# Two-layer cross attention: the opening and the batch ends of the second attention joined, and its tokens turned inside the first MLP's last weight group

## The chip, the cores and the metric

The kernel runs on one core of one Trainium2 chip. The metric is the device time of one launch in microseconds (us), lower is better. The core has five engines that run side by side and meet at semaphores: TensorE (PE; its weight loads are shown apart as PEld), VectorE (DVE), ScalarE (ACT), GpSimd (POOL) and SyncE (SP), whose queue issues most of the DMAs.

## The reference, cut to what matters

Four batches (B = 4) of 512 tokens with 512 features, a context of 64 tokens per batch, 16 heads of 32 features, all in float32. Two layers follow each other.

```python
# layer 0: tokens attend to the context, then an MLP
q = layer_norm(x) @ q_w + q_b;  k, v = ctx @ k_w + k_b, ctx @ v_w + v_b
x = softmax(mask(q k^T * HD**-0.5)) v @ cproj_w + cproj_b + x
x = x + gelu(layer_norm(x) @ fc_w + fc_b) @ proj_w + proj_b
# layer 1: the tokens are queries, keys are tokens AND context (512 + 64)
h = concatenate([latents, context]);  q = latents @ q_w + q_b;  kv = h @ kv_w + kv_b
attn = softmax(mask(q k^T / HD)) v            # one row sum per head and query
a = attn @ out_w + out_b + latents
out = gelu(rmsnorm(a) @ mlp_w1 + mlp_b1) @ mlp_w2 + mlp_b2 + latents
```

The latents of layer 1 are the tokens that layer 0 leaves. Both attention and MLP need them with the features on the partitions ("turned"), because PE sums over partitions.

## The kernel before, in words

The program is written engine by engine: each of the five has its own instruction stream, the orders are written out by hand, and semaphores tie them together. Each runs four stages: attention 0, MLP 0, attention 1, MLP 1. Every large product is made of three half products: an operand is split into a high part (`fp32r`) by ACT and a low part by DVE (`split_lo`, L1289), and high by high, high by low and low by high are summed in one PSUM bank. So a projection of a 128-row block is 12 matmuls of 512 columns (4 blocks of features by 3), and an evacuation of a bank is one ACT instruction and then one DVE instruction.

**MLP 0** goes through four groups of 512 hidden features; inside a group it goes through the four batches. A batch of a group is eight blocks of 12 matmuls: `fc1(0) fc1(1) fc2(0) fc1(2) fc2(1) fc1(3) fc2(2) fc2(3)`, 96 matmuls. Sums are kept in SBUF for all batches (`acc_`). Group 0 is written out batch by batch, with the norm and the turning of the next batch between the blocks (`turn_mlp`, 12 times four transposes); groups 1 to 3 are loops over the batches. When a batch of group 3 is done, SP stores its tokens to memory (`after_layer0`).

**Attention 1, opening** (before its loop): the tokens of batch 0 are in SBUF again; PE turns them (`nT0` to `nT3`, four transposes each) and the context (`nC`), projects queries, keys and context keys of head groups 0 and 1 (`nQ0 nK0 nKC0 nQ1 nK1 nKC1`) and the values (`nV0` to `nV4`). Queries and keys go through memory: SP stores the two parts (`q_parts`, `k_parts`) and loads them stacked, 32 rows per part, with a row of ones or of the mask beside them (`stack`). DVE sets the constant rows with memsets (L1629 to L1632). Then 20 `max_step`s find the row maxima of head group 0: a matmul to one of two banks and a DVE reduction from it. `max_turn` turns the maxima, SP moves them to a row of the queries (`max_row`), and the first scores can start.

**Attention 1, a batch**: four head groups (c = 0 to 3), each of 20 steps. A step has one score matmul, two exps on ACT (high and full), the low part on DVE or POOL, and two value matmuls four steps later. Between them stand the `max_step`s of the next head group and the "fillers": the projections for the head group after next. In c = 1 the fillers also hold `nT0` to `nT3` and `nC` of the next batch, at steps 12, 13, 15, 18 and 19. Batches 0 to 2 are one loop, batch 3 stands behind it.

**Batch end**: PE projects the next batch's values (`nV0` to `nV4`; the first two between the last value products). The 16 rows of sums, which SP has moved to `s16`, are inverted by one DVE reciprocal of 16x512; four matmuls (`B0` to `B3`, L2043) spread the inverses over the features; DVE multiplies (L1612), ACT adds the value bias in place (L1161), ACT and DVE split the result by blocks of tokens (L1165, L1289), and `O0` to `O3` (L2049, 48 matmuls) project it. In batch 3 the turning of MLP 1's first batch takes the place of the `nV`s.

All `n..`, `B` and `O` results share two PSUM banks in turn: result n waits until result n-2 has been evacuated (`free`). The order of results is the list from `results`.

## Time and profile before

| | |
|---|---|
| median of 3 runs | 1812.98 us (1812.66 to 1815.59) |
| the profiled execution | 1810.96 us, of which the span of its instructions is 1809.1 us |
| PE busy | 1623.9 us (90% of the span), 6993 matmuls |
| DVE, ACT, POOL busy | 1010.0, 699.9, 543.4 us |
| mean granted TensorE clock | 0.944 of full speed |

The share of busy time is a mean over stages with different limits, and PE's busy time is modelled: a matmul of 512 columns that stands alone is counted at about 0.4 us, in a stream its start follows the one before by 0.23 us. So the stages have to be read from the timeline, by when one piece of work starts and the next one starts. In the trace attention 1 begins at about 696 us, its loop at about 757 us; batch ends begin at about 895, 1064, 1236 and 1395 us.

### The profile page before, as it was taken

The page shows a single profiled execution, that of the slowest core. Times are in us where ns is not written, and L with a number is a line of the kernel's source. Part 1 is how long each engine was busy: PE and PEld are TensorE (multiplying, and loading weights), DVE is VectorE, ACT ScalarE, POOL GpSimd, SP SyncE. Part 2 cuts the span into 40 slices and gives each one's busy share as a digit, 9 for nine tenths or more (in the row PEclk, how much of TensorE's full clock was granted, in tenths as well). Part 3 has the DMA queues.
Part 4 walks back from the last instruction along what each step waited for, and adds up shares of the span by engine and source line. Part 5 has one row for each costly group of instructions (what it writes and reads, how often), then busy time and mean ns, then how long its engine had stood idle before and what let it go on. Part 6 is the DMA issues. An engine that isn't in the chain of part 4 may idle for free.

```text
span 1809.1 us, 23113 instructions
## 1 busy us (share of the span) xinstructions
PE 1623.9 (90%) x6993; PEld 1214.7 (67%) x6993; DVE 1010.0 (56%) x1612; ACT 699.9 (39%) x1260; POOL 543.4 (30%) x543
## 2 busy tenths in 40 slices
PE   5778897899999998899988998999887899999998
PEld 4667775677878786565655656665553577787886
DVE  3665565664333335488757866785877465333332
ACT  3433333341111111277557746673767232111111
POOL 3231236404040413234414423341457220404000
PEclk9888898999999998799989999899987799999999
DMA  5012013501010223423222322231222320101011
GB/s 181 1 36 70 23 51 125 191 13 47 0 47 0 68 96 120 130 84 109 82 71 78 111 63 103 71 106 59 91 86 71 139 77 12 35 12 35 0 47 46
DMA packets 60730, 126.13 MB, mean 70 GB/s; under 512 B 10397, under 2 KB 10722, under 8 KB 60642
## 3 DMA queue, kind: packets, MB, share of 16 engines
q1 hardware_dynamic: 53602, 102.08, 17.0%
q0 software_dynamic: 7040, 23.07, 4.1%
q8 instruction: 31, 0.51, 0.1%
q14 instruction: 57, 0.47, 0.1%
HBM read 90.25 MB, written 34.60 MB: 69 GB/s over the span
## 4 chain that ended last, share of the span: by engine, by line
PE 72%; DVE 13%; issue 7%; ACT 5%; DMA 2%; SPq 1%; POOL 1%; DVEq 0%; ACTq 0%; POOLq 0%
PE bank L2078 19%; PE bank L2090 18%; PE bank L1952 5%; DVE RA L1289 4%; PE bank L1948 3%; PE bank L2049 3%; DVE FA L1522 3%; PE bank L2002 3%; PE bank L1987 3%; PE bank L2003 2%; PE bank L1965 2%; PE bank L1774 2%; PE bank L1750 2%; PE bank L1969 2%; PE bank L1825 1%
## 5 line engine op out<-in xcount | busy, mean ns | idle before, releaser
L2090 PE MATMUL bank<-W,RA 128*128 128x512 f32 x1536 | 379.7, 399 | 5.9 <-DVE RA L1289 5.7
L2078 PE MATMUL bank<-RA,W 128*128 (+1 forms) x1536 | 374.8, 396 | 2.8 <-issue 2.3
L2090 PEld LDWEIGHTS bank<-W,RA 128*128 128x128 f32 x1536 | 287.2, 189 | 78.1 <-DVE RA L1289 10.7
L2078 PEld LDWEIGHTS bank<-RA,W 128*128 128x128 f32 x1536 | 286.9, 188 | 74.9 <-issue 6.0
L862 POOL TENSOR_TENSOR RA<-FA,RA 128x512 fp32r<-128x512 f32 (+1 forms) x160 | 216.0, 1354 | 392.9 <-ACT FA L1125 392.6
L1289 DVE TENSOR_TENSOR RA<-FA,RA 128x512 fp32r<-128x512 f32 (+2 forms) x308 | 273.3, 889 | 46.3 <-ACT FA L1125 32.6
L1181 ACT ACTIVATE FA<-bank,cols 128x512 f32<-128x512 f32 x128 | 88.1, 688 | 541.5 <-PE bank L2078 541.4
L1652 DVE CAST RA<-FA 128x512 fp32r<-128x512 f32 x128 | 62.8, 491 | 354.3 <-ACT FA L1181 354.3
L1124 ACT ACTIVATE RA<-bank 128x512 fp32r<-128x512 f32 (+1 forms) x320 | 193.6, 605 | 142.1 <-PE bank L1987 138.1
L1522 DVE TENSOR_REDUCE FA<-bank 128x1 f32<-128x512 f32 x256 | 169.1, 685 | 57.7 <-PE bank L1965 56.9
L1125 ACT ACTIVATE FA<-bank 128x512 f32<-128x512 f32 (+1 forms) x320 | 193.3, 604 | 0.0
L1987 PE MATMUL bank<-RA 98*128 98x512 f32 (+1 forms) x320 | 140.8, 442 | 14.8 <-DMA RA<-rows_ 7.2
L1952 PE MATMUL bank<-RA,W 128*128 128x512 f32 (+1 forms) x576 | 145.3, 370 | 5.1 <-DVE FA L1512 3.0
L2002 PE MATMUL bank<-RA 128*65 128x512 f32 (+1 forms) x320 | 136.9, 428 | 10.3 <-POOL RA L862 5.2
L1289 DVE TENSOR_TENSOR RA<-bank,RA 128x512 fp32r<-128x512 f32 (+1 forms) x124 | 82.9, 680 | 111.2 <-ACT RA L1105 43.0
L2003 PE MATMUL bank<-RA 128*65 128x512 f32 (+1 forms) x320 | 131.4, 411 | 0.0
L1952 PEld LDWEIGHTS bank<-RA,W 128*128 128x128 f32 x576 | 98.3, 197 | 40.5 <-issue 12.7
L721 POOL TENSOR_TENSOR W<-raw,W 128x512 fp32r<-128x512 f32 (+1 forms) x88 | 110.4, 1255 | 7.3
L1687 DVE TENSOR_TENSOR FA<-bank,FA 128x512 f32 (+1 forms) x128 | 86.8, 689 | 38.9 <-PE bank L2090 37.5
L1965 PE MATMUL bank<-RA 97*128 97x512 f32 x256 | 99.8, 430 | 6.4 <-DMA RA<-k_parts 2.0
L1987 PEld LDWEIGHTS bank<-RA 98*128 98x128 f32 (+1 forms) x320 | 60.1, 188 | 61.7 <-ACT FA L1125 35.2
L717 POOL TENSOR_SCALAR W<-raw 128x512 fp32r<-128x512 f32 (+1 forms) x88 | 56.4, 641 | 58.0 <-DMA raw<-in_L_xattn_mlp_w_dram 19.1
(149 smaller groups left out, 1828.7 us busy)
## 6 DMA issues: line engine op xcount, KB each, us to landing
RA<-k_parts SPq DMA_DIRECT2D x96, 144.0 KB
FA<-after_layer SPq DMA_DIRECT2D x12, 1024.0 KB, 6.1
RA<-q_parts SPq DMA_DIRECT2D x96, 128.0 KB
k_parts<-FA SPq DMA_DIRECT2D x16, 576.0 KB, 2.8
after_att<-FA SPq DMA_DIRECT2D x32, 256.0 KB, 2.1
q_parts<-FA SPq DMA_DIRECT2D x16, 512.0 KB, 2.7
raw<-in_L_xattn_mlp_w_dram POOLq DMA_DIRECT2D x32, 256.0 KB, 3.4
RA<-after_att SPq DMA_DIRECT2D x10, 512.0 KB, 6.9
```

The source lines that it names most:

```text
L862: pool.tensor_tensor(pl[0:m, r, :], pf[0:m, r, :], ph[0:m, r, :].bitcast(F32), ALU.subtract).then_inc(p_lo_pool, 1)
L1124: act.activation(ph[0:m, r, :], src, ACT.Exp, scale=SCALE1)
L1125: act.activation(pf[0:m, r, :], src, ACT.Exp, scale=SCALE1).then_inc(p_exp, 1)
L1289: dve.tensor_tensor(dst, src, hi.bitcast(F32), ALU.subtract).then_inc(sem_, 1)
L1522: dve.tensor_reduce(nm_main[:, TT * j + t:TT * j + t + 1], bank[2 + i % 2][:, :], AX_X, ALU.max, negate=True).then_inc(mm_free, 1)
L1952: op = pe.matmul(dst[:, 0:m], W[:, "QK".index(kind[0]), a, k, c * P:(c + 1) * P], src[:, d, k, :], start=start, stop=stop)
L1965: pe.matmul(bank[2 + i % 2][:, :], QS[0:ROWMAX, c % 2, j, t * P:(t + 1) * P], KS[0:ROWMAX, c % 2, j, 0:S], start=True, stop=True).then_inc ...
L1987: pe.matmul(bank[4 + n % 2][0:m, :], KS[0:ROWMAX + 1, c % 2, j, t * P:t * P + m], QS[0:ROWMAX + 1, c % 2, j, :], start=True, stop=True).th ...
L2002: pe.matmul(o, v, ph[0:m, n % PRING, :], start=(t == 0), stop=False)
L2003: pe.matmul(o, v, pl[0:m, n % PRING, :], start=False, stop=(t == TT)).then_inc(pv_step, 1)
L2078: op = pe.matmul(bank[FC1_BANK[i]][:, :], W[:, slot, a, k, i * P:(i + 1) * P], yT_[:, ds(b * (2 * KT * S) + (d * KT + k) * S, S)], start=( ...
L2090: op = pe.matmul(bank[4 + t][:, :], gs[:, a, i, t * P:(t + 1) * P], W[:, slot + 1, d, i, :], start=(i == 0 and a == 0 and d == 0), stop=(i ...
```

## The change

Five edits in one:

1. The last group of MLP 0 is no longer a loop: its four batches are written out on PE, ACT and DVE. In batches 1 to 3 PE turns the tokens of the batch before, straight from `acc_` (`x_turn`, four times four transposes, between the blocks). Batch 0's turned tokens are split to where attention 1 reads them; those of batches 1 and 2 are copied out by ACT (`x_out`) and stored turned (`x_store`, to `x_turned`). Batch 3 is turned in the opening of attention 1.
2. In c = 1 of the loop `nT0` to `nT3` are no PE work: the tokens come from memory turned; ACT copies them to the high part and DVE makes the low part, both from SBUF, at steps 12 to 15, `nC` at 16. PE waits for them (`x_split`) only at `nQ0`.
3. The opening: the constant rows come by eight DMAs during MLP 0 (`constant_rows1`); the parts of `nQ0` go to memory before those of `nKC0` are there; the 20 `max_step`s stand between the halves of `nV0` to `nV3`, and `nV4` behind `max_turn`; GpSimd asks for the first value weights before it waits for MLP 0's end; ACT has one `Exp` of a single column ahead of it all.
4. The batch end: the sums of heads 0 to 11 (`EARLY` = 12) are inverted apart, in four pieces, those of heads 12 to 15 in one piece of 16 partitions; `B0` to `B3` stand between `nV2`, `nV3` and `nV4`; bias and split are one ACT and one DVE instruction per block of features; `O0` starts with the first three blocks of features.
5. Batch 3: the early inverses, `B0` to `B2` and their products stand inside the last steps of c = 3; two of the four turnings stand ahead of `O0`.

```diff
-        plan += [(s0, 1, f"nT{k}") for k, s0 in enumerate((12, 13, 15, 18))] + [(19, 1, "nC")]
+        plan += [(s0, 1, f"nT{k}") for k, s0 in enumerate((12, 13, 14, 15))] + [(16, 1, "nC")]
...
-    out += [] if last else [f"nV{t}" for t in range(TT + 1)]
-    return out + [f"B{k}" for k in range(KT)] + [f"O{t}" for t in range(TT)]
+    out += [f"B{k}" for k in range(KT)] if last else ["nV0", "nV1", "B0", "nV2", "B1", "nV3", "B2", "nV4", "B3"]
+    return out + [f"O{t}" for t in range(TT)]
...
+def first_max(t, part):
+    at = 2 * t + part
+    return range((5 * at + 1) // 2, (5 * (at + 1) + 1) // 2)
+FIRST_X = {"nKC0": (0, 1), "nK1": (2, 3)}
... SP, opening
+                sp.wait_ge(rows_set, 16 * 8 + ONE)
                 for c in range(2):
+                    sp.wait_ge(pb_free, use1(f"nQ{c}", first=True) + 1 + ONE)
+                    parts(0, 0, c)
+                    if c == 0:
+                        for half in range(2):
+                            stack(0, c, half, (0,))
                     sp.wait_ge(pb_free, use1(f"nKC{c}", first=True) + 1 + ONE)
-                    parts(0, 0, c)
                     parts(1, 0, c)
-                    sp.wait_ge(consts, 5 + ONE)
                     for half in range(2):
-                        stack(0, c, half)
+                        stack(0, c, half, (1,) if c == 0 else (0, 1))
+                    if c == 0:
+                        for k in range(KT):
+                            x_store(B - 1, k)
... SP, MLP 0, last group
                 for b in range(B):
-                    if b == 2 and L.index == 0:
+                    if b >= 2 and L.index == 0:
+                        for k in range(KT):
+                            x_store(b - 1, k)
+                    if b == B - 1 and L.index == 0:
                         first_inputs1()
+                        constant_rows1()
... ACT
+            def x_out(nb, k):
+                act.wait_ge(x_full, KT * nb + k + 1 + ONE)
+                src = bank[3 if nb < B - 1 else 2 + k % 2][:, :]
+                if nb == 0:
+                    act.activation(xT[:, 0, k, :], src, ACT.Copy).then_inc(x_hi, 1)
+                else:
+                    v = KT * (nb - 1) + k
+                    if nb < B - 1 and v > 1:
+                        act.wait_ge(x_stored[k % 2], 16 * (v // 2) + ONE)
...
+                    act.activation(x_stage[nb][k], src, ACT.Copy).then_inc(x_moved, 1)
...
+                act.activation(cols[:, NPAR + 3:NPAR + 4], cols[:, NPAR:NPAR + 1], ACT.Exp)
                 for u in split_by_act(FIRST):
+                    for k in FIRST_X.get(u, ()):
+                        x_out(B - 1, k)
                     hi(0, u, first=True)
... DVE, end of a batch of the loop
+                        inverse(0)
+                        inverse(1)
                         lo(b, "nV0")
+                        inverse(2)
+                        inverse(3)
                         lo(b, "nV1")
-                    o_sum(H - 1)
+                        o_sum(H - 1)
+                        for k in range(2):
+                            scaled(k)
+                            as_lo_(k)
+                            lo(b, f"nV{k + 2}")
+                        inverse_last()
+                        scaled(2)
+                        as_lo_(2)
+                        lo(b, "nV4")
+                        scaled(3)
+                        as_lo_(3)
... PE
+            def x_turn(nb, k):
+                if k == 0:
+                    pe.wait_ge(acc_added, (NGRP - 1) * B * TT + (nb + 1) * TT + ONE)
+                pe.wait_ge(x_moved, KT * nb + k - (nb == B - 1 and k > 0) + ONE)
+                for t in range(TT):
+                    at_t = nb * TT * D + t * D + k * P
+                    op = pe.transpose(bank[3 if nb < B - 1 else 2 + k % 2][:, t * P:(t + 1) * P],
+                                      acc_[:, at_t:at_t + P], ident[:, :])
+                op.then_inc(x_full, 1)
... PE, end of a batch of the loop, then of batch 3
+                        spread_inverse(0)
+                        project(b, "nV2", 0, 1)
+                        spread_inverse(1)
+                        project(b, "nV3", 0, 1)
+                        spread_inverse(2)
+                        project(b, "nV4", 0, 1)
+                        spread_inverse(3)
+                        output(0, range(KT - 1))
                     else:
                         wait_apart(pe, (mm_free, at(0, b, BSTEP, BSTEP)))
+                        turn_mlp(LAYERS[1], 0, 0, 2)
+                        turn_mlp(LAYERS[1], 0, 1, 3)
+                        output(0, range(KT - 1))
+                        spread_inverse(3)
+                        for u in range(2, 4):
+                            evacuated(LAYERS[1], 0, u - 1)
                             turn_mlp(LAYERS[1], 0, u, 2 + u % 2)
+                    output(0, range(KT - 1, KT))
+                    for t in range(1, TT):
+                        output(t, range(KT))
... PE, opening
+                for u in FIRST[:FIRST.index("nV0")]:
+                    for k in FIRST_X.get(u, ()):
+                        x_turn(B - 1, k)
                     project(0, u, 0, 1, first=True)
+                pe.wait_ge(consts, 5 + ONE)
+                pe.wait_ge(x_moved, KT * B + ONE)
+                for t in range(TT):
+                    for part in range(2):
+                        for i in first_max(t, part):
+                            max_step(0, 0, i)
+                        project(0, f"nV{t}", part, 2, first=True)
                 max_turn(0, "nR0", 0, 0, first=True)
+                project(0, f"nV{TT}", 0, 1, first=True)
... PE, MLP 0, a batch of the last group (b > 0)
                     fc1(0)
                     fc1(1)
+                    x_turn(b - 1, 0)
                     fc2(0)
+                    x_turn(b - 1, 1)
                     fc1(2)
+                    x_turn(b - 1, 2)
                     fc2(1)
+                    x_turn(b - 1, 3)
```

On ACT `x_out` 0 and 1 stand between the gelus 1 and 2 of the batch and `x_out` 2 and 3 between the gelus 2 and 3; on DVE, in batch 1 alone, the low parts of batch 0's tokens (`x_lo`) stand in the same places. On DVE in batch 3 the four early inverses stand at steps 12 to 15 of c = 3 and the products of `B0` to `B2` at steps 17 to 19.

## Rows read from the trace of the kernel before

**Rows 1.** The page's head: the span.

```profile
span 1809.1 us, 23113 instructions
```

**Rows 2.** Stretches of time: length, busy time by engine (instructions), granted clock, DMA share, GB/s.

```profile
315.00:421.00 106.00, 96.08 (x423) 73.33 (x422) 61.52 (x109) 39.13 (x62) 22.53 (x24) 1.00 0.25 87
...
609.00:696.50 87.50, 87.12 (x375) 69.60 (x374) 32.32 (x47) 11.02 (x16) 24.00 (x34) 1.00 0.24 81
696.50:757.20 60.70, 48.70 (x186) 34.53 (x184) 34.60 (x47) 9.04 (x16) 23.87 (x36) 0.80 0.52 166
```

**Rows 3.** Timeline of the opening: start, length, engine, instruction, [idle before, releaser].

```profile
696.26 1.03 PE L1929 MATMUL bank<-ident,FA 128*128 128x128 f32 x8
...
701.84 8.63 PE L1952 MATMUL bank<-RA,W 128*128 128x512 f32 x36 [0.98 <-DVE RA L1289]
...
703.60 0.35 SPq L622 DMA_DIRECT2D brow<-in_L_xattn_out_b_dram  x1
...
716.20 0.34 SPq L535 DMA_DIRECT2D q_parts<-FA  x1
...
719.37 0.69 ACT L1097 ACTIVATE FA<-bank,cols 128x512 fp32r<-128x512 f32 x1 [8.54 <-DMA q_parts<-FA]
...
723.80 14.21 PE L1948 MATMUL bank<-W,RA 128*128 128x512 f32 x60 [0.35 <-issue]
...
754.36 0.37 PE L1976 MATMUL bank<-ident,FA 128*16 128x128 f32 x1 [0.77 <-issue]
...
757.19 1.21 PE L1987 MATMUL bank<-RA 98*128 98x512 f32 x2 [2.47 <-DMA RA<-rows_]
```

**Rows 4.** ACT's groups by line: the table loads ahead of exps.

```profile
L1124 ACT ACT_TABLE_LOAD x4 | 5.1, 1283 | 46.8 <-PE bank L1987 46.8
...
L978 ACT ACT_TABLE_LOAD x1 | 1.3, 1283 | 2.5 <-issue 2.5
```

**Rows 5.** Stretches: c = 1 of batches 0 to 3, then c = 3 of batch 3.

```profile
788.40:824.00 35.60, 31.21 (x148) 20.76 (x148) 27.79 (x43) 25.82 (x52) 13.90 (x11) 1.00 0.25 80
...
955.50:993.20 37.70, 33.53 (x148) 22.86 (x148) 27.89 (x43) 25.86 (x52) 13.67 (x11) 0.91 0.23 75
...
1124.90:1165.00 40.10, 35.58 (x146) 24.11 (x146) 28.89 (x43) 25.92 (x52) 13.07 (x11) 0.83 0.22 70
...
1294.40:1328.10 33.70, 30.40 (x131) 19.70 (x131) 27.40 (x40) 24.51 (x48) 13.49 (x11) 0.95 0.26 84
...
1359.90:1395.00 35.10, 25.08 (x71) 11.09 (x69) 26.94 (x32) 26.86 (x52) 32.42 (x27) 0.81 0.15 54
```

**Rows 6.** PE's timeline in c = 1 of batch 2.

```profile
1155.09 1.12 PE L1929 MATMUL bank<-ident,FA 128*128 128x128 f32 x4 [1.65 <-DVE FA L1512]
```

**Rows 7.** DVE's groups, shapes apart, in c = 1 of batch 0: busy, mean ns.

```profile
L1289 DVE TENSOR_TENSOR RA<-FA,RA 128x512 fp32r<-128x512 f32 x9 | 8.5, 948 | 0.7 <-ACT FA L1125 0.6
...
L1289 DVE TENSOR_TENSOR RA<-bank,RA 128x512 fp32r<-128x512 f32 x3 | 2.0, 682 | 0.0
```

**Rows 8.** Timeline of the end of batch 0.

```profile
895.06 8.64 PE L1948 MATMUL bank<-W,RA 128*128 128x512 f32 x36
...
899.62 3.34 DVE L1592 RECIPROCAL FA<-FA 16x512 f32<-16x512 f32 x1
...
903.93 1.09 PE L2043 MATMUL bank<-FA,rows_ 16*128 16x512 f32 x2 [0.23 <-DVE RA L1289]
...
912.06 14.00 PE L2049 MATMUL bank<-W,RA 128*128 128x512 f32 x48 [3.19 <-DVE RA L1289]
...
925.90 0.63 PE L1987 MATMUL bank<-RA 98*128 98x512 f32 x2
```

**Rows 9.** Timeline of the end of batch 3 and the start of MLP 1.

```profile
1395.05 1.51 PE L1714 MATMUL bank<-ident,FA 128*128 128x128 f32 x8
...
1413.39 14.20 PE L2049 MATMUL bank<-W,RA 128*128 128x512 f32 x48 [3.14 <-DVE RA L1289]
...
1428.58 5.83 PE L2078 MATMUL bank<-RA,W 128*128 128x512 f32 x24 [0.98 <-issue]
```

More of the change, by code:

```diff
@@ L200, in at, with program @@
     return b * per + (base + max(n, 0) + ONE)
-def program(nc, x, ctx, mask_bool, mask_int, w, x1, xm, x2, q_parts, k_parts, out):
+def program(nc, x, ctx, mask_bool, mask_int, w, x1, xm, x2, q_parts, k_parts, x_turned, out):
     es = ExitStack()
@@ L1198, in mlp @@
                 for g in range(1, NGRP):
-                    with act.Fori(0, B) as b:
-                        batch(b, g, False)
+                    if L.index == 0 and g == NGRP - 1:
+                        for b in range(B):
+                            batch(b, g, False)
+                    else:
+                        with act.Fori(0, B) as b:
+                            batch(b, g, False)
             act.wait_ge(consts, 2 + ONE)
@@ L1691, in mlp @@
                 for g in range(1, NGRP):
-                    with dve.Fori(0, B) as b:
-                        batch(b, g, False)
+                    if L.index == 0 and g == NGRP - 1:
+                        for b in range(B):
+                            batch(b, g, False)
+                    else:
+                        with dve.Fori(0, B) as b:
+                            batch(b, g, False)
             attention0()
@@ L2018, in batch @@
                                 project(b, u, part, n, last)
+                            if not ahead and i >= 17:
+                                spread_inverse(i - 17)
                             if ahead and i == TURN:
@@ L2125, in mlp @@
                     pe.wait_ge(w_lo, L.before + L.units + (g + 1) * 2 * KT + ONE)
-                    with pe.Fori(0, B) as b:
-                        batch(b, g, False)
+                    if L.index == 0 and g == NGRP - 1:
+                        for b in range(B):
+                            batch(b, g, False)
+                    else:
+                        with pe.Fori(0, B) as b:
+                            batch(b, g, False)
             attention0()
```

292 lines of the change are left out of this document (189 added, 103 removed).

## The prediction

> **What bounds the kernel now.** I read the head first: the span is 1809.1 us [rows 1], the profiled execution 1810.96. That leaves 1.9 us outside the span, which I keep. The execution is 2.0 us under the median of 1812.98, so I add 2.0 at the end.
>
> Then the stretches. In the last group of MLP 0 PE is busy for 87.1 of 87.5 us at the full clock [rows 2]: there an added PE instruction costs its own time. The opening (696.5 to 757.2) is the opposite: 60.7 us, no engine busy throughout, clock at 0.80 on average [rows 2]. It is a chain of hand-overs, and the same holds for the batch ends [rows 8, 9]. The stages between are mixed: in c = 1 PE, DVE and ACT are all busy for 70 to 90% [rows 5]. So I price every edit by its stage, from "this starts" to "the next thing starts".
>
> **The change part by part.**
>
> *1. MLP 0, last group.* Three batches get four turns of four transposes, 12 turns. The opening shows two such turns in 1.03 us [rows 3], 0.52 each: 12 x 0.52 = 6.2. The copies on ACT (11.0 us busy in 87.5), the low parts on DVE (32.3) and the stores stand in engines that are mostly idle here [rows 2]; a turn waits for the copy of the one before, which has 12 matmuls to get done. What hides them is gone if a copy is late; then gelu 2 is late behind it. Written out instead of looped: I take nothing. Bounds: from 4 (turns that overlap the stream a little) to 18.5, the length by which group 0, which has 12 such turns and the norm, exceeds this one (106.0 against 87.5 [rows 2]). I take **+6**, as the added work has no norm.
>
> *2. Opening.* Before: MLP 0 ends at 696.26, projections start at 701.84, `q_parts` leaves at 716.20 because SP waits for `nKC0`, the values run from 723.80 to 738.01, the 20 max steps to 754.36, the first scores start at 757.19 [rows 3]. After: the context is turned at once, projections start at about 698.4 (estimate: one ACT, one DVE instruction). SP is free at 703.60, as it still waits for batch 3's store [rows 3]; `q_parts` follows, landing takes 3.2 (716.20 to 719.37), six loads to issue 2.7 (estimate, at 0.34 to 0.5 each), `k_parts` again 3.5, key loads and mask row about 4: 717.3. PE's own work to that point (24 full and 12 small matmuls, twice, 8.6 each [rows 3], and two pairs of turns, 1.03 each) ends at about 717 too. Max steps and `nV0` to `nV3` then share PE: alone they take 16.3 and 11.4 (4/5 of 14.21), so 16.3 if they overlap fully, 27.7 if not; I take 19, since half a value projection fits into the wait for a reduction. `max_turn` to first scores takes 2.8 [rows 3], and the low part of `nV3` is now queued on DVE ahead of it, 0.7 and a hand-over: 740.2. For stretches at the lower clock I add 2: 742.2 instead of 757.2, **-15**. The constant rows and the early dummy `Exp` lie under MLP 0's last matmuls; the value weights come about 3 earlier and are not waited for. Bounds: -20 (full overlap, no slow clock) to -5 (no overlap, load chain 2 later).
>
> *3. Table load.* In each round of the loop the first exp waits for a table load of 1.28 us after the scores are there; with one more after batch 3's square root that makes the four of [rows 4]. The `Exp` ahead of the loop makes the table the same on both ways into it. In attention 0 a loop of two rounds that is entered with the exp table has no load at its first exp: only the exp ahead of the loop has one (x1, [rows 4]). So three go: 3 x 1.28 = **-3.9**; bounds 0 and -3.9. The Trainium skill (ScalarE activation tables: per-element evaluation and per-set limits, section Table sets in the compiler and the runtime) says that loads are placed per block. Read strictly, the loop body is a block and keeps its load, and the term is 0; the row of attention 0 speaks against that reading.
>
> *4. c = 1.* The stage took 35.6, 37.7 and 40.1 in the three rounds; in batch 3, without `nT` and `nC`, 33.7 [rows 5]. PE stood still for up to 1.65 us ahead of an `nT` [rows 6], in order, so the scores behind it were late too, and in the third round the clock fell to 0.83. After, PE has only `nC`. ACT and DVE keep their instructions, so I don't take 33.7 but 34.0: 113.4 - 102 = **-11**. But the low parts now read two SBUF operands. Such ones took 948 ns here, those with one operand in PSUM 682 [rows 7]: 12 x 0.27 = 3.2 if all of it shows. Bounds: -12.3 (33.7 each) to +3.2 (no stall was on the path). The Trainium skill (SBUF — State Buffer, section Who interferes with whom) has the reason: a DVE instruction with two SBUF inputs excludes a GpSimd one that reads SBUF, and the later one stands still. By that the low parts of the probabilities on GpSimd would be late as well, which speaks against this edit.
>
> *5. Batch ends 0 to 2.* Before: 895.06 to 925.90, 30.8 us [rows 8]: `nV2` to `nV4` 8.6, the inverses spread after that, splits, 3.19 of waiting, `O` 14.0 at a clock that had partly fallen. The other two have the same pattern. After, on PE: 8.64 + four spreads of 1.09 + 48 matmuls at the pace of the 36 (0.24), 11.5: 24.5. Joined results wait for the bank of the result before last: its evacuation, ACT 0.69 and DVE 0.68 [rows 3, 7] with hand-overs 1.5, against one spread of 1.09 between, and DVE has products and splits in between: 0.6 ahead of each of `nV3`, `nV4`, `O0`, 1.9 in all: 26.4, that is -4.4 each, **-13.2**. The reciprocal of 3.34 becomes four quarters and one more of 0.84; the first two fill DVE's wait for `nV0`, the others that for `nV1`. Late next is the bank pair. Bounds each: -6.3 (no bank wait) to +4.2 (seven waits of 1.5 in full: 24.5 + 10.5).
>
> *6. Batch 3.* Before: 1395.05 to 1428.58, 33.5 [rows 9]. After: two turns 1.5; `O0` begins when ACT has done the last head and three splits (4 x 0.69) and DVE the last low part (0.7), with hand-overs at 1398.9, three matmuls more 1399.8; `B3` 1.1; the other two turns with an evacuation between 2.1: 1403.0; the remaining 39 matmuls at 14.20/48 = 0.30 each [rows 9] 11.5; the step to MLP 1 1.0: 1415.5, -13. In c = 3 DVE gets 3.34 + 3 x 0.68 = 5.4 more where it is busy for 26.9 of 35.1 us [rows 5]: 0 to 5.4, I take 2.5. **-10.5**; bounds -17 (full clock in `O`, DVE hidden) to 0.
>
> *Sum:* 6 - 15 - 3.9 - 11 - 13.2 - 10.5 = -47.6. 1810.96 - 47.6 = 1763.4, and with 2.0 to the median **1765**.
>
> **The rivals.**
>
> *A. The lock outweighs the stall in c = 1.* DVE and ACT already bound that stage; PE's stalls were slack, and the slower low parts add 3.2. For it: DVE is busy for 27 to 29 us there [rows 5]. Against: 33.7 in the round without `nT`. Then the term is +3.2 instead of -11: 1779.
>
> *B. The load stays in the loop.* 1765 + 3.9 = 1769.
>
> *C. Joining only trades one wait for another.* Two banks serve spreads, values and outputs; each waits out an evacuation, and the opening stays behind the load chain. Ends 0, opening -5, batch 3 -5: 6 - 5 - 3.9 - 11 - 5 = -18.9: 1794. For it: every joined result has the same two banks. Against: a spread or a projection always lies between two uses of a bank.
>
> *D. Slower: the last MLP group loses its clock.* Each turn waits for the sums of the batch before and for the copy of the last turn; if PE stands at them, the clock falls from 2.4 to 1.2 GHz as in c = 1 (0.83 in the third round [rows 5]), and a batch of some 22 us (87.5/4) takes 44. Three batches: +66, 1831. It decides from 47.6/22 = 2.2 batches on. Against: group 0 has 12 turns in the same places and a clock of 1.00 [rows 2].
>
> *E. The change moves the turns and saves none.* As many transposes come to MLP 0 as leave attention 1, and PE was the bound in both: part 4 gives 6.2 instead of 11: 1770.
>
> **How the numbers follow.** Forecast 0.60, A 0.13, B 0.09, C 0.08, D 0.03, E 0.07. The parts' bounds taken together are wider than I believe; the best ones that go together (4, -20, -3.9, -12.3, -18.9, -15) give -66 and 1747; I take 1745 as the low end. The high end reaches to C and stops short of D: 1792. The measurement can tell about 0.2% (3.6 us) from no change. Faster: all but D and a tail of C in which two terms turn positive, 0.94; within 0.2% 0.02; slower 0.04.
>
> **What would show it.** In the profile of the changed kernel: the last MLP group at 93 to 95 us and a clock of 1.00 (D wrong); from the last `fc2` to the first scores about 46 us, max steps and values interleaved over some 19; the first exp of each round without a load (B wrong); c = 1 at about 34 in every round with DVE's low parts of the tokens near 0.95 us (A wrong); the ends at about 26, with PE's waits ahead of `nV3`, `nV4` and `O0`; `O` in batch 3 ending some 12 us earlier behind the last value product. The prediction is wrong if the opening's load chain is later than 720, if PE waits at every spread, or if a turn in MLP 0 costs more than 1 us.

## The result, and the profile after

The kernel before took 1814.3 us (median of four runs beside the changed kernel, 1812.7 to 1817.5), the changed kernel 1783.7 (1781.7 to 1786.6): ratio 0.983, 95% interval 0.981 to 0.985. That is 30.6 us less, where 47.6 were forecast and 1765 us predicted. The profiled execution after took 1786.58 us, 24.4 less than the profiled one before.

The head of the page of the changed kernel, against [rows 1]:

```profile
span 1784.7 us, 23062 instructions
```

Two stretches of it, the last group of MLP 0 and the opening, with the columns of [rows 2] (length, busy time by engine, granted clock, DMA share, GB/s):

```profile
609.10:704.80 95.70, 95.24 (x434) 76.53 (x432) 35.74 (x53) 19.03 (x30) 25.73 (x38) 1.00 0.27 96
704.80:755.40 50.60, 39.31 (x186) 30.43 (x186) 19.67 (x36) 8.01 (x15) 22.71 (x34) 0.90 0.69 211
```

From its first to its last matmul the group took 90.3 us before ([rows 2] cuts some 3 us into it) and takes 95.6 now, 5.3 more, and PE stays at the full clock: rival D is out. The opening is 10.1 us shorter, with a DMA share of 0.69 instead of 0.52.

The opening on the timeline, against [rows 3]:

```profile
711.00 0.32 SPq L556 DMA_DIRECT2D q_parts<-FA  x1
...
714.56 0.28 DVE L1620 SCALAR_TENSOR_TENSOR FA<-bank,cols,FA 128x64 fp32r<-128x64 f32 x1 [1.01 <-ACT FA L1174]
...
715.88 2.96 SPq L567 DMA_DIRECT2D RA<-q_parts  x6
...
719.04 0.34 SPq L556 DMA_DIRECT2D k_parts<-FA  x1
...
725.10 1.25 SPq L567 DMA_DIRECT2D RA<-k_parts  x3
...
728.96 1.19 PE L2118 MATMUL bank<-RA 97*128 97x512 f32 x2 [6.98 <-DMA RA<-rows_]
...
751.00 0.27 PE L2129 MATMUL bank<-ident,FA 128*16 128x128 f32 x1
...
755.42 0.63 PE L2140 MATMUL bank<-RA 98*128 98x512 f32 x2
```

Read it backwards: the interleaved part takes 22.0 (728.96 to 751.00), and ahead of it PE stands for 7 us, waiting for the key loads and the constant row issued behind them. The key parts are ready on DVE at 714.84, but SP stores them only at 719.04: it first waits until the query parts have landed (4.9 us, not 3.2) and issues six query loads.

ACT's table loads ahead of exps, against [rows 4] (L1248 is the dummy, L1196 the exps of the second attention):

```profile
L1248 ACT ACT_TABLE_LOAD x1 | 1.3, 1283 | 0.0
L1196 ACT ACT_TABLE_LOAD x1 | 1.3, 1283 | 0.0
```

The one that is left at L1196 is the one behind batch 3's square root.

Stages c = 1 and c = 2 of the three rounds, cut at the issue of the row of maxima (`max_row`; the expectations below call it the mask row). They are shown in pairs because that row is later now, so that the cut itself moves:

```profile
783.12:820.46 37.34, 30.96 (x138) 19.69 (x138) 30.86 (x46) 29.16 (x59) 15.03 (x12) 0.99 0.24 76
820.46:852.81 32.35, 28.61 (x124) 19.48 (x124) 25.09 (x38) 21.43 (x42) 11.45 (x9) 0.91 0.40 120
948.79:984.92 36.13, 32.75 (x138) 20.21 (x138) 30.57 (x45) 28.11 (x57) 14.76 (x12) 0.93 0.26 78
984.92:1016.98 32.06, 28.59 (x125) 19.36 (x124) 24.55 (x38) 22.41 (x44) 11.47 (x10) 0.92 0.39 121
1112.78:1149.01 36.23, 32.93 (x138) 20.34 (x138) 30.59 (x45) 28.19 (x57) 14.79 (x12) 0.93 0.26 78
1149.01:1180.96 31.95, 28.51 (x125) 19.23 (x124) 24.54 (x38) 22.40 (x44) 11.47 (x9) 0.92 0.39 121
```

The same pair in the first round before:

```profile
787.88:823.45 35.57, 31.18 (x145) 20.42 (x146) 27.32 (x43) 25.79 (x52) 14.30 (x11) 1.00 0.25 80
823.45:854.69 31.24, 29.09 (x135) 19.19 (x133) 26.23 (x41) 24.29 (x49) 12.65 (x11) 1.00 0.38 124
```

The pairs sum to 69.7, 68.2 and 68.2 now; before they were 66.8, 68.9 and 71.5. PE has fewer instructions. DVE has 2.4, 1.4 and 0.4 us more than in the same round before, and c = 2, at the full clock in all rounds before, stands at 0.91 to 0.92. Two of PE's waits in the first round's c = 1 before (us in total, times, longest):

```profile
PE bank L1929 <- DVE FA L1512: 2.6, 2, 1.3
PE bank L1969 <- DVE FA L1522: 0.7, 1, 0.7
```

The same stage now, then c = 2:

```profile
PE bank L2122 <- DVE FA L1630: 2.0, 2, 1.4
```

```profile
PE bank L2140 <- DMA RA<-rows_: 3.0, 1, 3.0
```

PE's waits have moved. Those ahead of the turns (2.5 to 2.8 us a round) are gone, but the maximum steps (L2122, before L1969) wait longer for DVE's reductions, and the first scores of c = 2 wait for the row of maxima: 3.0, 1.6 and 1.6 us, at most 0.4 before. DVE's low parts with two SBUF operands, against [rows 7], c = 1 of the first round; the four of the tokens are among the 13:

```profile
L1386 DVE TENSOR_TENSOR RA<-FA,RA 128x512 fp32r<-128x512 f32 x13 | 12.1, 941 | 0.9 <-ACT FA L1197 0.9
```

The end of batch 0 on PE, against [rows 8], and that of batch 3, against [rows 9]:

```profile
893.14 1.12 PE L2175 MATMUL bank<-FA,rows_ 12*128 12x512 f32 x2
894.19 3.07 PE L2101 MATMUL bank<-W,RA 128*128 128x512 f32 x12
...
908.06 11.45 PE L2164 MATMUL bank<-W,RA 128*128 128x512 f32 x48 [0.61 <-DVE RA L1386]
919.34 0.63 PE L2140 MATMUL bank<-RA 98*128 98x512 f32 x2
...
1382.77 1.09 PE L1862 MATMUL bank<-ident,FA 128*128 128x128 f32 x8
...
1391.14 9.34 PE L2164 MATMUL bank<-W,RA 128*128 128x512 f32 x39 [0.35 <-issue]
...
1401.47 2.79 PE L2261 MATMUL bank<-RA,W 128*128 128x512 f32 x11 [0.98 <-issue]
```

The first takes 26.2 us (893.14 to 919.34; forecast 26.4, before 30.8), the second 18.7 (before 33.5).

### The profile page after: what moved, and what is told of

Same layout as the page of the kernel before. It is cut to its first block, busy times and chain, and to the rows that moved or that the text cites. A ratio compares the mean times of both kernels' runs of the same rounds, so it can differ in the third digit from the quotient of the medians.

```text
span 1784.7 us, 23062 instructions
## 1 busy us (share of the span) xinstructions
PE 1605.2 (90%) x7017; PEld 1198.8 (67%) x7017; DVE 1019.4 (57%) x1625; ACT 696.8 (39%) x1255; POOL 545.5 (31%) x543
## 4 chain that ended last, share of the span: by engine, by line
PE 71%; DVE 13%; issue 7%; ACT 4%; DMA 3%; SPq 1%; POOL 0%; DVEq 0%; ACTq 0%; POOLq 0%
PE bank L2261 18%; PE bank L2273 18%; PE bank L2105 5%; DVE RA L1386 4%; PE bank L2155 3%; PE bank L2101 3%; PE bank L2140 3%; PE bank L2156 3%; DVE FA L1630 3%; PE bank L2164 3%; PE bank L2118 2%; PE bank L1922 2%; PE bank L1898 2%; PE bank L2122 2%; PE bank L1973 1%
## 5 line engine op out<-in xcount | busy, mean ns | idle before, releaser
L2261 PEld LDWEIGHTS bank<-RA,W 128*128 128x128 f32 x1536 | 286.5, 188 | 74.5 <-issue 6.1
L1386 DVE TENSOR_TENSOR RA<-FA,RA 128x512 fp32r<-128x512 f32 (+2 forms) x304 | 282.1, 930 | 40.0 <-ACT FA L1197 33.1
L1196 ACT ACTIVATE RA<-bank 128x512 fp32r<-128x512 f32 (+1 forms) x320 | 192.7, 602 | 162.8 <-PE bank L2140 156.7
L2140 PE MATMUL bank<-RA 98*128 98x512 f32 (+1 forms) x320 | 141.7, 445 | 16.1 <-DMA RA<-rows_ 10.5
L2155 PE MATMUL bank<-RA 128*65 128x512 f32 (+1 forms) x320 | 139.8, 437 | 6.7 <-DVE RA L1386 4.9
L2105 PE MATMUL bank<-RA,W 128*128 128x512 f32 (+1 forms) x576 | 140.3, 359 | 1.0 <-DVE RA L1386 1.0
L2156 PE MATMUL bank<-RA 128*65 128x512 f32 (+1 forms) x320 | 134.3, 420 | 0.0
L1386 DVE TENSOR_TENSOR RA<-bank,RA 128x512 fp32r<-128x512 f32 (+1 forms) x112 | 74.8, 679 | 86.3 <-ACT RA L972 31.3
L2105 PEld LDWEIGHTS bank<-RA,W 128*128 128x128 f32 x576 | 94.6, 191 | 34.1 <-issue 10.6
L2140 PEld LDWEIGHTS bank<-RA 98*128 98x128 f32 (+1 forms) x320 | 60.3, 189 | 68.9 <-ACT FA L1197 33.6
```

Source lines behind the costliest of these rows:

```text
L1196: act.activation(ph[0:m, r, :], src, ACT.Exp, scale=SCALE1)
L1386: dve.tensor_tensor(dst, src, hi.bitcast(F32), ALU.subtract).then_inc(sem_, 1)
L2105: op = pe.matmul(dst[:, 0:m], W[:, "QK".index(kind[0]), a, k, c * P:(c + 1) * P], src[:, d, k, :], start=start, stop=stop)
L2140: pe.matmul(bank[4 + n % 2][0:m, :], KS[0:ROWMAX + 1, c % 2, j, t * P:t * P + m], QS[0:ROWMAX + 1, c % 2, j, :], start=True, stop=True).th ...
L2155: pe.matmul(o, v, ph[0:m, n % PRING, :], start=(t == 0), stop=False)
L2156: pe.matmul(o, v, pl[0:m, n % PRING, :], start=False, stop=(t == TT)).then_inc(pv_step, 1)
```

## The experiments

All stages below are read in the same way, in one profile per kernel: c = 1 and c = 2 from one row of maxima to the next, the opening from the last `fc2`'s end to the first scores.

**Table loads alone (`tables_only`).** The kernel before, with

```
+                act.activation(cols[:, NPAR + 3:NPAR + 4], cols[:, NPAR:NPAR + 1], ACT.Exp)
                 for u in split_by_act(FIRST):
                     hi(0, u, first=True)
                 with act.Fori(0, B - 1) as b:
```

> The kernel before with one edit: the dummy Exp ahead of the loop of the second attention. My theory: the table is then the same on both ways into the loop, so the group of table loads ahead of the exps falls from x4 to x1, no load stands behind the scores of a round any more, and each of the three stages c = 0 is 1.28 us shorter: some 3.9 us less in all (1.6 to 4 with what the scatter of single runs does to it). Rival (the load is placed per block, so the loop keeps it): still x4, no change. Besides, the profile of this kernel has MLP 0 and MLP 1 with the code of the kernel before a second time: if their lengths differ by 2 to 3 us from the first profile (290.4 us from MLP 0's start to its last group, 369.2 for MLP 1), the 2.4 and 2.8 us that these unchanged parts were longer in the profile of the changed kernel are scatter and not an effect of the change.

Measured: ratio to the kernel before 0.997 (0.995 to 1.000), 1 to 9 us less, so the times of the runs have room for the 3.9 and the stages must decide. The loads are gone as expected (x4 to x1), but of the 3.9 us the stages show only 1.5: 0.8 in the first c = 0 (32.81 to 32.05) and 0.7 in the next two rounds together, which took 29.0 and 30.4 from the first scores to the row of maxima before and 29.4 and 29.4 here. First the start of the second round before, then the same place here:

```profile
926.61 1.28 ACT L1124 ACT_TABLE_LOAD   x1 [13.87 <-PE bank L1987]
...
929.38 0.69 DVE L1289 TENSOR_TENSOR RA<-FA,RA 128x512 fp32r<-128x512 f32 x1 [2.59 <-ACT FA L1125]
```

```profile
929.71 0.60 ACT L1124 ACTIVATE RA<-bank 128x512 fp32r<-128x512 f32 x1 [13.35 <-PE bank L1988]
...
931.96 1.30 POOL L862 TENSOR_TENSOR RA<-FA,RA 128x512 fp32r<-128x512 f32 x1 [37.30 <-ACT FA L1125]
...
932.19 1.61 DVE L1290 TENSOR_TENSOR RA<-FA,RA 128x512 fp32r<-128x512 f32 x1 [2.32 <-ACT FA L1125]
```

With the load gone the exp starts at once, 0.7 us after the scores. But DVE still begins its first low part 2.3 to 2.5 us after its last sum, much as before (the bracket: 2.59, and 2.33 in the third round), and now beside GpSimd's, so that it takes 1.61 instead of 0.69. At the entry to batch 3, where no loop is closed, DVE comes 0.77 us after its last sum in both kernels. So, as far as these places show, the load lay beside DVE's way back to the top of the loop. The Trainium skill (Runtime: NRT & Kernel Launch, section Instruction fetch mechanics) says that a taken branch out of the fetched window costs a fetch of its target; the 2.3 us agree with that, and no run here shows the fetch itself.

The profile also served as a second one of unchanged code. MLP 0 from start to last `fc2` took 377.7 and 377.8 in the two kernels without turns in it; MLP 1 to the end of the span 380.5 and 378.3, and in the ten experiments below 379.2 to 381.4, against 383.2 in the changed kernel's. The 2.8 us that MLP 1 seemed to lose there is scatter.

**c = 1: low parts left out (`c1_low_left_out`).** The changed kernel, with

```
-    split_lo(xT[:, 1, k, :], tokT[:, k, :], xT[:, 0, k, :], x_split)
+    split_lo(xT[:, 1, k, 0:16], tokT[:, k, 0:16], xT[:, 0, k, 0:16], x_split)
```

> The changed kernel with the low parts of the turned tokens made for 16 columns instead of 512 (the rest is left out, so the tokens of batches 1 to 3 have wrong low parts); all waits stay. Theory: in c = 1 DVE is full from the first low part on, the joined maximum stands behind them, the mask row leaves late, and the first score of c = 2 waits up to 3 us for it with a lower clock behind. Then c = 1 falls from 37.3, 36.1 and 36.2 to about 34 in each round, c = 2 from 32.1 to about 31.3, and the total by 8 to 11 us. Rival (ACT with its four copies, or PE with the context's turn, sets the stage): c = 1 stays within 0.7 of 36 and the total within 3 us.

Measured: 1781.8 us, ratio 0.982 (0.979 to 0.984). The pairs were 67.2, 67.2 and 67.2, below all fifteen rounds with the changed code (68.1 to 72.6). Neither theory: 1.0 to 2.5 us per round come back, but c = 1 is 34.4 to 36.1, not 34. The second round:

```profile
946.50:981.35 34.85, 31.93 (x136) 20.16 (x136) 28.60 (x45) 27.62 (x56) 13.99 (x11) 0.94 0.25 81
981.35:1013.68 32.33, 30.09 (x128) 19.99 (x127) 24.53 (x38) 22.94 (x45) 12.03 (x10) 0.91 0.37 120
```

DVE is 2 us less busy in c = 1 (28.6 for 30.6), ACT as busy as in the changed kernel (27.6 for 28.1), and the clock still falls; in this round and the third, c = 2 has no wait for the row of maxima. The low parts are a part of the cause, not all of it.

**c = 1: low parts on GpSimd (`c1_low_on_pool`).** In DVE's loop `nT` is skipped; in GpSimd's

```
+    if not last and 14 <= n - NSTEP < 14 + KT:
+        k = n - NSTEP - 14
+        wait_apart(pool, (act_out, at(0, b, SPLITS, split1(f"nT{k}", last) + 1)))
+        pool.tensor_tensor(xT[:, 1, k, :], tokT[:, k, :], xT[:, 0, k, :].bitcast(F32), ALU.subtract)...
```

> The changed kernel with the four low parts of the turned tokens on GpSimd instead of VectorE, at steps 14 to 17 of c = 1. Theory (VectorE's queue is the bound, GpSimd is busy for 13.5 of 36 us there): c = 1 at 34 to 35, c = 2 at 31.5, total 5 to 9 us less. Rival (two engines that both read two operands from SBUF stand in each other's way, so it does not matter which of them does the low parts): c = 1 stays at 36 or more, the low parts of the probabilities on GpSimd are late and values wait for them, total within 2 us or longer.

Measured: 1782.9 us, ratio 0.982 (0.981 to 0.984). The pairs were 69.7, 68.8 and 69.0: the rival's outcome, though not its reason, which this run does not show. GpSimd's busy time in the first round's c = 1 rose from 15.0 to 17.9 us, DVE's fell from 30.9 to 28.5, and nothing was gained.

**c = 1: the same work later (`c1_late`).** `nC` at step 12, `nT0` to `nT3` at steps 16 to 19, and in c = 2 the query and key projections two steps later:

```
-    spans = ((1, 5), (6, 5), (11, 1)) if turns else ((1, 6), (7, 5), (12, 1))
+    spans = ((1, 5), (6, 5), (11, 1)) if turns else ((3, 5), (8, 5), (13, 1)) if c == 2 else ((1, 6), (7, 5), (12, 1))
...
-        plan += [(s0, 1, f"nT{k}") for k, s0 in enumerate((12, 13, 14, 15))] + [(16, 1, "nC")]
+        plan += [(s0, 1, f"nT{k}") for k, s0 in enumerate((16, 17, 18, 19))] + [(12, 1, "nC")]
```

> The changed kernel with the turned tokens' high and low parts four steps later in c = 1 (steps 16 to 19, behind the joined maximum and its turn on VectorE), the context's turn at step 12, and the query and key projections of c = 2 two steps later. c = 1 and c = 2 together took 69.7, 68.2 and 68.2 in the changed kernel, 66.8, 68.9 and 71.5 in the kernel before, 67.2 three times with the low parts left out. Theory (VectorE's order makes the mask row late; TensorE then waits and its clock falls from 1.00 to 0.50 for some 7 us around the end of c = 1): the mask row leaves 2 us earlier, no wait of 3 us at the first score of c = 2, the granted clock stays at 1.00 there, and the sum falls to 66 to 67, total 4 to 7 us less. Rival (VectorE has that much to do in c = 1 and c = 2 together, 55 of 68 us, and the order only moves the gap): the sum stays at 68 to 69.5 and the clock falls elsewhere in c = 2.

Measured: 1794.8 us, ratio 0.989 (0.983 to 0.995), the slowest of the c = 1 runs. The pairs were 71.3, 68.8 and 70.4. My theory of the order alone fell: c = 1 of the first round took 38.95 us at a clock of 0.79, and in the third the loss moved into c = 2 (36.86).

**c = 1: no work on the tokens at all (`split_kept`).** The high and low parts are both made in the last group of MLP 0 (batch 3's in the opening), kept in memory, and loaded into place in c = 1:

```
-        plan += [(s0, 1, f"nT{k}") ...] + [(16, 1, "nC")]
+        plan += [(13, 1, "nC")]
... ACT, DVE in MLP 0 and the opening
+    act.activation(x_stage[nb][k].bitcast(F32R), src, ACT.Copy).then_inc(x_hi, 1)
+    split_lo(lo_stage[nb][k], src, x_stage[nb][k], x_moved)
... SP, c = 1, behind the store of the key parts
+    if c == 1 and not last:
+        sp.dma_start(xT_.bitcast(F32)..., x_turned[ds(b + 1, 1), :, :, :, :]...).then_inc(x_loaded, 16)
```

> The changed kernel with the turned tokens kept in memory as their high and low parts, both made inside the last group of MLP 0 (for batch 3 in the opening) and loaded straight into place in c = 1, 2 MB at once, behind the third key projection. So c = 1 loses four copies of 0.6 us on ScalarE and four low parts of 0.95 us on VectorE; what is left for the next batch is the context's turn, at step 13. Theory (VectorE and ScalarE bind c = 1 and c = 2, TensorE's turns were slack, so the change took away what cost nothing and kept what costs): c = 1 and c = 2 together fall from 68.2 to 69.7 to 65.5 to 67, total 4 to 9 us less than the changed kernel. Rival one (TensorE's clock falls in the new gaps): 67 to 68.5. Rival two (2 MB don't land between step 12 of c = 1 and the query projection of c = 2): TensorE waits for the load there, the sum is 69 or more. In the last group of MLP 0 eight low parts more lie on VectorE, busy for a third there: 0 to 1 us.

Measured: 1791.4 us, ratio 0.987 (0.985 to 0.989). Slower than the changed kernel in all, but for a reason of its own: c = 1 took 33.2, 32.3 and 32.5 us at a clock of 1.00, the shortest so far, and c = 2 took 39.8, 38.3 and 38.2. The timeline around the end of c = 1:

```profile
813.14 0.37 SPq L623 DMA_DIRECT2D RA<-x_turned  x1
...
816.37 0.55 SPq L574 DMA_DIRECT2D RA<-rows_  x1
...
826.12 0.77 PE L2149 MATMUL bank<-RA 98*128 98x512 f32 x1 [8.51 <-DMA RA<-rows_]
```

The 2 MB load took 12.1 us to land (10.4 and 9.7 in the other rounds), and the row of maxima, 8 KB on the same queue, landed behind it, 9.6 us after its issue. PE's waits for it were 8.5, 6.6 and 5.9 us. Rival two had the wait right and its place wrong: not the load at the projections was waited for, but what stood behind it in the queue.

**The opening: key parts first (`open_k_first`).** The changed kernel, with

```
     parts(0, 0, c)
-    if c == 0:
-        for half in range(2):
-            stack(0, c, half, (0,))
     sp.wait_ge(pb_free, use1(f"nKC{c}", first=True) + 1 + ONE)
     parts(1, 0, c)
     for half in range(2):
-        stack(0, c, half, (1,) if c == 0 else (0, 1))
+        stack(0, c, half)
```

> The changed kernel with the old order of the loads in the opening: the key parts are stored as soon as they are there (VectorE has them at 714.8), ahead of the six query loads, which in the changed kernel stand before them in SP's queue, wait for the query parts to land and hold the key parts back to 719.04. Theory: the key parts leave at about 715.2, land at 720 to 721, the key loads leave at about 721 and the first maximum step starts at about 724.5 instead of 728.96; first scores 3.5 to 4.5 us earlier. Rival (the landing is slow because the transfers share the engines: value weights, query loads and stores together): the key parts leave early but land late, and the first maximum step comes less than 1.5 us earlier. A second rival: the values' weights, there at 726.9, hold the interleaved chain back; then half of the gain is lost.

Measured: 1784.9 us, ratio 0.984 (0.981 to 0.987), opening 51.4: no gain, by the second rival. The `fc2` ends at 702.45:

```profile
712.65 0.32 SPq L556 DMA_DIRECT2D k_parts<-FA  x1
...
723.59 1.19 PE L2115 MATMUL bank<-RA 97*128 97x512 f32 x2 [3.98 <-DMA RA<-rows_]
...
727.47 0.74 POOL L771 TENSOR_TENSOR W<-raw,W 128x256 fp32r<-128x256 f32 x1
...
728.36 2.90 PE L2098 MATMUL bank<-W,RA 128*128 128x512 f32 x6 [2.42 <-POOL W L771]
```

The first maximum step is 21.1 us behind the `fc2` instead of 24.1, but the first value product then waits for GpSimd's last weights. Their loads took 5.2 us instead of 4.2, and the weights were there 25.8 us behind the `fc2` instead of 22.1: the first rival's reason holds for them.

**The opening: weights earlier too (`open_early`).** The same edit, and the first split of the value weights waits for the last `fc1` of MLP 0, not for the last `fc2`:

```
     if i and u == 0:
-        pool.wait_ge(a_full, its + ONE)
+        pool.wait_ge(f_full, NGRP * NCH * B + ONE)
... put_o
+    if u == 0:
+        pool.wait_ge(a_full, its + ONE)
```

> The changed kernel with two edits in the opening: the key parts are stored ahead of the query loads (alone it brought the first maximum step from 24.1 to 21.1 us after the last fc2, but the first value product then waited 2.42 us for GpSimd's weights, first scores at 51.4 as without it), and the value weights' first split waits for the last fc1 instead of the last fc2, some 5.8 us earlier. Theory (loads and weights bound the opening side by side): the weights are there at 16 to 20 us, the first step at 21 to 22, 22 us of interleaved work without a wait for weights, first scores at 46.5 to 48.5, 3 to 4 us less than in the changed kernel. Rival (the transfers of weights, query and key parts share the DMA engines, so what one gains the others lose): first step at 23 or later, first scores within 1.5 us of 51.

Measured: 1779.4 us, ratio 0.982 (0.975 to 0.989), opening 47.9 as the theory had it. The interval holds the changed kernel's 0.983 too, so the gain is read from the opening alone. The `fc2` ends at 702.47:

```profile
717.10 0.75 POOL L771 TENSOR_TENSOR W<-raw,W 128x256 fp32r<-128x256 f32 x1
...
723.09 0.73 PE L2117 MATMUL bank<-RA 97*128 97x512 f32 x2 [3.45 <-DMA RA<-rows_]
...
745.94 0.27 PE L2128 MATMUL bank<-ident,FA 128*16 128x128 f32 x1
```

The weights are there 5 us ahead of the first step, and the interleaved work runs without a wait for them, 22.9 us.

**The opening: values, then maximum steps (`open_values_first`).** The changed kernel, with the order as before:

```
     for t in range(TT):
-        for part in range(2):
-            for i in first_max(t, part):
-                max_step(0, 0, i)
-            project(0, f"nV{t}", part, 2, first=True)
+        project(0, f"nV{t}", 0, 1, first=True)
+    for i in range(NSTEP):
+        max_step(0, 0, i)
```

> The changed kernel with the values and maximum steps of the opening one after the other, as before: nV0 to nV3, then the 20 steps. In the changed kernel it is 50.6 to 51.5 us from the last fc2 to the first scores: first maximum step at 24.1 us, 22.0 of interleaved work, 4.4 to the first scores. Theory (interleaving saves): the values start when their weights are there, about 22.5, take 11.4 to 13, the steps 16.3, then 2.8 to 4: first scores at 53.5 to 56, 3 to 5 us more. Rival (the late loads and weights set the opening, the order does not matter): at most 1.5 us more, since values first fill the wait for the key loads.

On DVE the low parts and the reductions follow the same order. Measured: 1791.6 us, ratio 0.988 (0.982 to 0.994), opening 57.9, 6.4 to 7.3 more than interleaved; the theory's direction, and more than it said. The values waited until 22.3 us for their weights, took 13.7 and not 11.4, and `nV4` ran for 5.3 us at half the clock.

**Batch ends taken apart (`ends_apart`).** On PE, with ACT and DVE in the same order:

```
-    spread_inverse(0)
-    project(b, "nV2", 0, 1)
-    ... to spread_inverse(3)
+    for t in range(2, TT + 1):
+        project(b, f"nV{t}", 0, 1)
+    for k in range(KT):
+        spread_inverse(k)
```

> The changed kernel with the batch ends of the loop taken apart again: nV2 to nV4 first, then the four spreads, then the output; the quarter reciprocals, the splits by 128 channels and the two banks stay. From the mask row of c = 0 (nR0) to the first scores of the next batch it took 38.2 to 39.8 us before and 34.8 in all four profiles with the changed code. Theory (the joining itself fills the waits for the two banks): 37.5 to 38.5 again, 8 to 11 us more in all. Rival (the gain comes from the smaller pieces, four reciprocals that lie in VectorE's idle time and one split per block of 128 channels instead of add, copy and split): at most 1 us more per end, total within 3 us of the changed kernel.

Measured: 1793.0 us, ratio 0.987 (0.981 to 0.993). From the row of maxima to the first scores it took 37.1, 37.0 and 37.0, against 34.8 joined and 39.8, 38.5 and 38.2 before. Both theories hold a part: 2.2 us per end from joining, 1.9 on average from the smaller pieces.

**Two edits together.** The kernel without work on the tokens in c = 1 (`split_kept`), with the opening whose weights come earlier too (`open_early`).

> The kernel split_kept with the opening of open_early (key parts stored ahead of the query loads, value weights from the last fc1 on; first scores 47.9 instead of 50.6 to 51.5 us after the last fc2, as measured). If the two edits add up, it is 3 us below split_kept; with the theory of split_kept some 1770 to 1776 us, ratio to the kernel before 0.977 to 0.980. If the low parts of batch 3's tokens on VectorE delay the key parts in the opening, 1 to 2 us of that are lost.

Measured: 1789.6 us, ratio 0.986 (0.983 to 0.988). The opening was 45.6 for 50.4 in `split_kept`, but c = 2 had the same wait (38.2 to 39.5). The opening's gain came in full. What it is above 3 us is not shown to be more than scatter: the same opening took 47.9 in `open_early` and 47.6 in the kernel below. The number expected had left out the queue, as that of `split_kept` had.

**The load earlier (`split_early_open`).** The same kernel, the 2 MB load right behind the query loads of c = 1:

```
     pair(0, (0,))
+    if c == 1 and not last:
+        wait_apart(sp, (pb_full, at(0, b, USES, use1("K3", last) + 1)))
+        sp.dma_start(xT_.bitcast(F32)..., x_turned[ds(b + 1, 1), :, :, :, :]...).then_inc(x_loaded, 16)
     wait_apart(sp, (pb_free, at(0, b, USES, use1(f"{pre}KC{nc_}", last) + 1)))
     parts(1, nb, nc_)
```

> The kernel split_kept_open with the 2 MB load of the tokens' two parts some 7 us earlier: as soon as TensorE has done the third key projection (step 10 of c = 1), ahead of the key parts, instead of behind them. In split_kept the load went out at 813.14, took 12.1 us and held the mask row (816.37) back in the queue: the first scores of c = 2 waited 8.5 us, c = 2 took 38 to 40, and c = 1 took 32.3 to 33.2 at the full clock. Theory (the mask row only stands behind the load): the load goes out at about 806, lands at 818, the wait at the first scores of c = 2 falls to 1 to 2 us, c = 1 and c = 2 together 64.5 to 66, total 1767 to 1775, ratio to the kernel before 0.973 to 0.979. Rival (the load, wherever it stands in the queue, delays the key parts and their loads, which the maximum steps of c = 2 need): TensorE waits for the key loads in c = 2 instead, the sum stays at 68 or more.

Measured: 1766.6 us (1759.3 to 1770.9), ratio 0.973 (0.970 to 0.975), the fastest of all: against the changed kernel's 0.983 another 1.0%, some 18 us (the two were timed beside the kernel before, not beside each other). About 15 lie in the pairs, which are 64.5, 64.9 and 63.6, and 3 in the opening (47.6). The load went out at 802.52 and landed in 7.8 us; PE waited 0.7 us for the row of maxima and 0.6 for key loads, so the rival is out. The first round:

```profile
779.40:812.48 33.08, 29.47 (x136) 19.58 (x135) 26.48 (x40) 24.66 (x50) 13.05 (x11) 1.00 0.43 150
812.48:843.87 31.39, 28.61 (x129) 18.76 (x127) 25.83 (x39) 23.82 (x48) 13.05 (x11) 1.00 0.39 123
```

Against the changed kernel DVE has 3.6 us less in the pair (52.3 for 55.9), ACT 2.1 less, PE 1.5 less at a full clock, and the pair is 5.2 us shorter.

## Why the prediction was right and wrong

*The last group of MLP 0 (+6): right.* MLP 0 as a whole took 377.7 and 377.8 us without the turns and 383.3 to 387.3 with them, median 383.9 over eight profiles: 6.2 us.

*The opening (-15): a third of it did not come.* Measured -9.3 to -10.2. The order of the load chain was right: landing, six issues, key parts, key loads. Its landings were mis-sized. That of the query parts was taken from the quieter opening before (3.2 us [rows 3]) and took 4.9; for the key parts "`k_parts` again 3.5" was taken, and they landed 6.1 after their issue. That the streams hinder each other is not shown by itself; the DMA share of 0.69 for 0.52 goes with it. So the first step came at 24.1 us behind the `fc2`, for some 21 forecast (717.3 against 696.3) and past the prediction's own sign of being wrong (720, that is 23.7). The order in SP's queue cost besides that the key parts left 4.2 us after they were ready. The interleaving took 22.0 for 19, of which the 2 us added for the lower clock cover most, and was worth 6 to 7 us, as the run without it shows. `open_k_first` and `open_early` show that two chains, loads and weights, ended within some 2 us of each other (24.1 and 22.1): freeing the loads alone gave nothing, freeing both gave 3 us, and the weights alone were not tried.

*Table loads (-3.9): three loads went, 1.5 us came.* Rival B (the load stays) is refuted by the row x1. The Trainium skill (ScalarE activation tables: per-element evaluation and per-set limits, section Table sets in the compiler and the runtime) says that loads are placed per block; here a loop body that is entered and left with the exp table kept none. The failed step is a different one: that what the load delays is late by the load's whole length. DVE began its first low part 2.3 to 2.6 us after its last sum with the load and 2.3 to 2.5 without it.

*c = 1 (-11): nothing.* Over c = 1 and c = 2 the mean of six rounds was 68.8 us before (two profiles) and 69.3 in fifteen rounds with the changed code (five profiles). The step that failed is "in order, so the scores behind it were late too": that PE's stalls ahead of the turns set the stage. They were slack, as rival A had it, whose 1779 is the nearest of the forecasts: PE no longer waits for the turns, but waits as long for DVE's reductions and for the row of maxima. What stayed were ACT's copies and DVE's low parts, now in four steps ahead of that row. The comparison with batch 3 (33.7 [rows 5]) misled: that round lacks the copies and low parts too, not only the turns. Taking away all of it (`split_early_open`) gave 5.0 us a round (64.3 on average), the low parts alone 2. How much of the rest is ACT's was not tried by itself. The clock made it worse: in c = 2 it was 1.00 in all rounds before, 0.91 to 0.92 in the changed kernel, and 1.00 again in `split_early_open`. The wait for the row of maxima alone does not explain it. With the low parts left out, c = 2 stood at 1.00 in the first round, where that wait was 2.4 us, and at 0.91 and 0.89 in the other two, which had none. What decides it is open. Rival A's reason, the shared port, is borne out only in single places: the Trainium skill (SBUF — State Buffer, section Who interferes with whom) lets such a DVE instruction and a GpSimd one exclude each other, and DVE's 1.61 us beside GpSimd's 1.30 agrees; but the mean of the low parts is 941 ns, for 948 before, and moving them to GpSimd changed nothing.

*Batch ends (-13.2): right.* 34.8 for 39.8, 38.5 and 38.2: -12.2 over three ends. About half is the joining, the other half the pieces; rival C is refuted. In the first end PE waited 0.47, 0.47 and 0.61 us ahead of `nV3`, `nV4` and `O0`, where the forecast had 0.6 each: the mechanism held too.

*Batch 3 (-10.5): right in the sum, in the profiled pair.* The end took 14.8 less (13 forecast), as `O` ran at 0.24 us a matmul and not 0.30, and c = 3 took 4.3 more (2.5 forecast): 36.4 to 40.8 us from the turn of its maximum to the first token turn, with DVE busy for 32.1 of 39.6 us where it had been 26.9 of 35.1 [rows 5], and the granted clock at 0.74 for 0.81. That the two misses cancel is luck of this profile: c = 3 and the end together took 70.0 and 68.4 us in the two kernels without the change and 58.3 to 64.1 in the eleven with it, 61.0 on average, some 8 less.

*The rest.* Of the 23 us between forecast and profiled pair some 11 are in c = 1 to c = 3, 5 in the opening, and 5 in MLP 0 and MLP 1, in code that was not changed; the second profiles show most of those 5 to be the scatter of one execution. The medians lie 17 apart.

## What to carry to other kernels

A stall on one engine is worth something only if nobody else would be late without it: before pricing it, take the engines' work of the whole stage, and compare with a stage that lacks just the instructions that go. Where two chains end close together, as loads and weights here, shorten both or expect nothing. And a big transfer is priced by what stands behind it in its queue: behind 2 MB an 8 KB row was waited for 8.5 us, and 0.7 once the 2 MB went out 7 us earlier.

## What the runs showed of the hardware that was not expected

An 8 KB transfer issued 3.2 us behind a 2 MB one on SP's queue (`split_kept`) landed just behind it: 9.7 us from its issue to the first scores, where the changed kernel's opening shows 2.6. Stores of 512 and 576 KB landed after 4.9 and 6.1 us in the opening at a DMA share of 0.69, and after 3.2 and 4.0 at 0.52. And around PE's gaps at the end of c = 1 the granted clock went from 1.00 to 0.50 (2.4 to 1.2 GHz) and up again in the changed kernel's first round; slices of 3.4 us:

```profile
813.72:817.12 3.40, 2.64 (x14) 1.34 (x13) 3.34 (x6) 2.98 (x7) 1.11 (x1) 1.00 0.45 172
817.12:820.52 3.40, 1.95 (x7) 0.74 (x7) 3.37 (x8) 2.91 (x7) 1.31 (x2) 0.86 0.00 0
820.52:823.92 3.40, 1.52 (x4) 1.05 (x5) 1.86 (x2) 0.79 (x3) 0.63 (x1) 0.50 0.46 123
823.92:827.32 3.40, 3.40 (x11) 2.34 (x10) 1.19 (x2) 2.19 (x5) 1.28 (x1) 0.64 0.85 213
```

DVE is full in the first two (3.34 and 3.37 of 3.4), and PE's waits there are for DVE's reductions and their join; in the third PE waits for the row of maxima.
